# A value product that takes two chunks of keys at a time, and an order of work that prices the change of kind

## What is computed

```python
def attn(q, k, v, heads):            # per example and head, dh = 160 // heads
    sim = q @ k.T * dh ** -0.5
    return softmax(sim, axis=-1) @ v

x = attn(x Wq, ctx Wk, ctx Wv, 20) Wo + bo + x                # unit 0, cross
for block in (L1, L3):
    h = ln(x); x = attn(h q1, h k1, h v1, 20) o1 + x          # units 1 and 5, self
    h = ln(x); x = attn(h q2, ctx k2, ctx v2, 20) o2 + x      # units 2 and 6, cross
    h = ln(x); x = (a * gelu(g)) ff_w2 + x                    # a, g = h ff_w1
    # between L1 and L3 stands L2: 8 heads of 20, keys 508 rows of the context (unit 3),
    # and a small attention of 96 queries over the 256 rows of x (unit 4, "ca")
```

## Time and profile before

| what | value |
|---|---|
| the three runs | 1089.43, 1079.00, 1082.56 us |
| their median | 1082.56 us |
| the profiled execution | 1083.78 us |
| its span on the core | 1082.0 us |
| granted clock, mean of the span | 0.981 |

### The profile page before, as it was taken

One profiled execution on the slowest core, in us unless ns is written; L12 is line 12 of the kernel. 1 busy time (PEld: TensorE's weight loads), 2 busy tenths in 40 slices (PEclk: granted clock), 3 DMA queues, 4 the chain that ended last, 5 costly groups with the idle time before them and its releaser, 6 DMA issues.

```text
span 1082.0 us, 21250 instructions
## 1 busy us (share of the span) xinstructions
PE 1034.7 (96%) x7808; PEld 719.5 (67%) x7808; DVE 689.4 (64%) x1603; ACT 675.4 (62%) x1400; POOL 74.0 (7%) x129
## 2 busy tenths in 40 slices
PE   8999989999998999999998998999999899999978
PEld 5656666667685666767685666676768566765646
DVE  3777757875546567875755775787555556777631
ACT  4556666766664666766765665776665556766641
POOL 3000000000002100001010000000100110000000
PEclk9899999999999999999999999999999999999995
DMA  8110001110232101010113010101021400111000
GB/s 195 42 39 17 21 22 44 30 31 11 49 77 56 25 21 45 21 31 22 35 31 89 21 26 20 45 21 31 10 60 30 103 20 22 34 25 40 11 7 7
DMA packets 31150, 40.26 MB, mean 37 GB/s; under 512 B 10324, under 2 KB 22232, under 8 KB 30728
## 3 DMA queue, kind: packets, MB, share of 16 engines
q1 hardware_dynamic: 31048, 38.89, 14.9%
HBM read 10.97 MB, written 0.66 MB: 11 GB/s over the span
## 4 chain that ended last, share of the span: by engine, by line
PE 87%; DVE 5%; ACT 4%; issue 3%; DMA 0%; POOLq 0%; POOL 0%; DVEq 0%; ACTq 0%
PE st_ps L775 18%; PE pv_ps L831 17%; PE mx_ps L794 17%; PE sp_ps L757 8%; PE sp_ps L758 7%; PE sp_ps L876 4%; PE sp_ps L858 3%; DVE mx L1221 2%; PE sp_ps L808 2%; PE sp_ps L950 2%; PE sp_ps L938 2%; PE sp_ps L989 2%; ACT probs L1062 2%; ACT oT L1069 1%; PE sp_ps L893 1%
## 5 line engine op out<-in xcount | busy, mean ns | idle before, releaser
L1221 DVE TENSOR_REDUCE mx<-mx_ps 128x1 f32<-128x512 f32 (+2 forms) x720 | 475.4, 685 | 184.4 <-PE mx_ps L794 181.1
L1062 ACT ACTIVATE probs<-st_ps 128x512 f32<-128x512 f32 x720 | 400.6, 597 | 184.3 <-PE st_ps L775 178.4
L794 PE MATMUL mx_ps<-ring,qT 128*128 128x512 f32 (+2 forms) x864 | 294.9, 400 | 6.9 <-issue 3.8
L775 PE MATMUL st_ps<-qT,ring 128*128 128x256 f32 (+1 forms) x1408 | 276.1, 298 | 5.4 <-ACT probs L1062 3.2
L775 PEld LDWEIGHTS st_ps<-qT,ring 128*128 128x128 f32 (+1 forms) x1408 | 217.8, 190 | 80.4 <-ACT probs L1062 40.6
L831 PE MATMUL pv_ps<-probs,v 128*9 128x256 f32 (+3 forms) x2944 | 223.8, 377 | 3.0 <-ACT probs L1062 2.3
L794 PEld LDWEIGHTS mx_ps<-ring,qT 128*128 128x128 f32 x864 | 143.5, 190 | 88.9 <-DVE mx L1221 45.7
L831 PEld LDWEIGHTS pv_ps<-probs,v 128*9 128x9 f32 (+2 forms) x2944 | 44.9, 90 | 64.3 <-issue 19.2
L1111 ACT ACTIVATE kdense<-sp_ps 128x512 f32<-128x512 f32 (+2 forms) x116 | 57.4, 539 | 24.4 <-PE sp_ps L876 23.9
L1049 ACT ACTIVATE ks<-sp_ps 128x320 fp32r<-128x320 f32 x80 | 35.2, 440 | 42.3 <-PE sp_ps L858 27.5
L876 PE MATMUL sp_ps<-identr,ks 128*128 128x128 f32 (+1 forms) x416 | 59.7, 279 | 0.7 <-DVE qs L1187 0.6
(11 more groups left out here) (134 smaller groups left out, 1050.2 us busy)
## 6 DMA issues: line engine op xcount, KB each, us to landing
ring<-kdense SPq DMA_DIRECT2D x256, 64.0 KB, 2.0
wb<-in_w_blk SPq DMA_DIRECT2D x4, 1400.0 KB, 9.1
ring<-kdense SPq DMA_DIRECT2D x160, 32.0 KB, 1.8
ring<-kdense SPq DMA_DIRECT2D x32, 127.0 KB, 2.3
wd<-in_w_down SPq DMA_DIRECT2D x4, 400.0 KB, 9.5
ring<-oT SPq DMA_DIRECT2D x16, 64.0 KB, 3.2
ctx_n<-in_ctx SPq DMA_DIRECT2D x4, 192.0 KB, 6.6
x<-in_x SPq DMA_DIRECT2D x4, 160.0 KB, 3.3
```

The source lines that it names most:

```text
L775: mm = pe.matmul(st_ps[s % N_ST][0:kr, i * a["nq"]:(i + 1) * a["nq"]], key_op(n, h)[:, c * P:c * P + kr], query_op(u, b)[:, h // of(u), :] ...
L794: mm = pe.matmul(mx_ps[o % N_MX][0:rows, j * a["nk"]:(j + 1) * a["nk"]], query_op(u, b)[:, h // of(u), tt * P:tt * P + rows], key_op(n, h) ...
L1062: nc.scalar.activation(probs[0:kr, s % N_P, 0:w], st_ps[s % N_ST][0:kr, 0:w], ACT.Exp, scale=float(a["dh"]) ** -0.5).then_inc(S["probs_rea ...
L1221: nc.vector.tensor_reduce(mx[b][0:rows, t, heads[0]:heads[-1] + 1], mx_ps[(o - 1) % N_MX][0:rows, 0:a["hpm"] * a["nk"]].rearrange("p (h k) ...
```

## The change

A value product covers `RUN` = 2 chunks: `runs(u)` gives pairs of chunks, every use of a chunk's number in `plan`, `simulate`, `build` and the TensorE program goes by pairs. Every unit has an even number of chunks, so 368 steps `pv` become 184, each of 16 records. The step waits for the exp of its last slot (the fourth, in unit 4 the second), and each slot still signals by itself when it has been read. `probs` has 7 buffers. In `cost`, `st`, `max` and `pv` have other values, and `simulate` adds `MODE` = 95 ns where a step of TensorE is of another kind (`pv`: "columns", else: "full") than the one before it.

```diff
-N_P = 6
+N_P = 7
 RING = 4
+RUN = 2
 PV_LAG = 2
...
+def runs(u):
+
+    n_c = -(-ATT[u]["nk"] // P)
+    return [list(range(c, min(c + RUN, n_c))) for c in range(0, n_c, RUN)]
...
-        for c in range(q["n_c"]):
-            last = max(s for s in q["slots"] if slots[s]["c"] == c)
-            put(last + PV_LAG, 2, ("pv", n, c))
+        for i, cs in enumerate(runs(q["u"])):
+            last = max(s for s in q["slots"] if slots[s]["c"] == cs[-1])
+            put(last + PV_LAG, 2, ("pv", n, i))
...
-        return 4 + 0.417 * rows, [("dve", 60 + 1.05 * rows)]
+        return 4 + 0.45 * rows, [("dve", 60 + 1.05 * rows)]
...
-        return 218, act(512)
+        return 236, act(512)
     if kind == "pv":
-        return 4 * nq * 0.47, []
+        return len(runs(u)[step[2]]) * nq * 1.57, []
...
+MODE = 95
...
     clock = dict(pe=0, act=0, dve=0, pool=0, dma=0)
+    mode = "full"
+
+    def shape(step):
+
+        return "columns" if step[0] == "pv" else "full"
+
+    def pe_free(step):
+
+        return clock["pe"] + (0 if shape(step) == mode else MODE)
+
...
-            key = (max(start, clock["pe"]), due.get(step)) if cost(step, quads)[0] else (max(start, clock["pe"]), (-10**6, 0, 0))
+            key = (max(start, pe_free(step)), due.get(step)) if cost(step, quads)[0] else (max(start, clock["pe"]), (-10**6, 0, 0))
...
-            t = clock["pe"] = max(start, clock["pe"]) + pe
+            t = clock["pe"] = max(start, pe_free(step)) + pe
+            mode = shape(step)
...
                     elif kind == "pv":
-                        _, n, c = step
+                        _, n, k = step
...
-                        mine = [s for s in quads[n]["slots"] if slots[s]["c"] == c]
-                        if c == 0 and n:
+                        n_c = -(-a["nk"] // P)
+                        mine = [s for s in quads[n]["slots"] if slots[s]["c"] in runs(u)[k]]
+                        if k == 0 and n:
                             pe.wait_ge(S["out_taken"], n)
                         pe.wait_ge(S["probs_ready"], slot_value("probs_ready", mine[-1]))
...
-                        kr = chunk_rows(a["nk"], c)
                         for s in mine:
+                            c = slots[s]["c"]
+                            kr = chunk_rows(a["nk"], c)
                             for i, h in enumerate(slots[s]["heads"]):
...
-                                               start=(c == 0), stop=(c == -(-a["nk"] // P) - 1), tile_position=(0, 32 * j))
-                            if s == mine[-1] and c == -(-a["nk"] // P) - 1:
+                                               start=(c == 0), stop=(c == n_c - 1), tile_position=(0, 32 * j))
+                            if slots[s]["last"]:
                                 mm.then_inc(S["out_full"], 1)
                             else:
                                 mm.then_inc(s_used, 1)
```

More of the change, by code:

```diff
@@ L325, in simulate @@
             streams[4].append(("clear", n))
-        streams[3] += [("pv", n, c) for c in range(q["n_c"])] + [("oev", n)]
+        streams[3] += [("pv", n, i) for i in range(len(runs(q["u"])))] + [("oev", n)]
     last_of, produced = {}, {}
@@ L332, in simulate @@
     for q in quads:
-        for c in range(q["n_c"]):
+        for i, cs in enumerate(runs(q["u"])):
             for s in q["slots"]:
-                if slots[s]["c"] == c:
-                    pv_of[s] = ("pv", q["n"], c)
+                if slots[s]["c"] in cs:
+                    pv_of[s] = ("pv", q["n"], i)
     def needs(step):
@@ L357, in needs @@
         if kind == "pv":
-            return ([("st", max(s for s in quads[step[1]]["slots"] if slots[s]["c"] == step[2]))]
+            cs = runs(quads[step[1]]["u"])[step[2]]
+            return ([("st", max(s for s in quads[step[1]]["slots"] if slots[s]["c"] == cs[-1]))]
                     + ([("oev", step[1] - 1)] if step[1] and step[2] == 0 else []))
         if kind == "oev":
-            return [("pv", step[1], quads[step[1]]["n_c"] - 1)]
+            return [("pv", step[1], len(runs(quads[step[1]]["u"])) - 1)]
         if kind == "kv_proj":
@@ L487, in build @@
         kinds = {step[0]}
-        if step[0] == "pv" and step[2] == -(-ATT[quads[step[1]]["u"]]["nk"] // P) - 1:
+        if step[0] == "pv" and step[2] == len(runs(quads[step[1]]["u"])) - 1:
             kinds.add("pv_last")
@@ L608, in build @@
                 for s in quads[step[1]]["slots"]:
-                    if slots[s]["c"] == step[2]:
+                    if slots[s]["c"] in runs(quads[step[1]]["u"])[step[2]]:
                         if slots[s]["last"]:
@@ L812, in _ @@
                     elif kind == "pv":
-                        _, n, c = step
+                        _, n, k = step
                         u, b, qd = quads[n]["u"], quads[n]["b"], quads[n]["qd"]
                         a = ATT[u]
-                        mine = [s for s in quads[n]["slots"] if slots[s]["c"] == c]
-                        if c == 0 and n:
+                        n_c = -(-a["nk"] // P)
+                        mine = [s for s in quads[n]["slots"] if slots[s]["c"] in runs(u)[k]]
+                        if k == 0 and n:
                             pe.wait_ge(S["out_taken"], n)
                         pe.wait_ge(S["probs_ready"], slot_value("probs_ready", mine[-1]))
-                        if c == 0 and qd == 0:
+                        if k == 0 and qd == 0:
                             last = [s for s in order if s[0] in ("kv_proj", "qkv_proj", "x_keys") and
```

## The result

The changed kernel takes 1120.56 us (median of four runs, 1115.42 to 1123.1) against 1081.9 of the kernel before (median of four runs, one more than ahead of the prediction): 1.034 times as long, 95% interval 1.0275 to 1.0405. The forecast was 1043 us. The profiled execution of after took 1115.42 us with a span of 1113.6. Some executions of a kernel have a clearly lower granted clock and take over 1.5% longer than its fastest; medians and ratios leave them out.

A forecast was written before the change was run, and what follows sets the result against it. TensorE was taken as the bound: span 1082.0 - 49 for fewer changes + 9 for new waits = 1042, plus 1.8 around it and less 1.2 for the median, gave 1043 us, range 1035 to 1053.

The forecast's parts named there:

- Fewer changes: On TensorE, 180 changes to column tiles and back go at 0.30 us each: 54 us, 49 on the chain.
- Longer blocks: A run holds TensorE 1.00 us; full banks give 1.09 us of exp and 1.29 of reduction, covering both engines.
- the 9 us for all new waits: Allowance in the sum for TensorE's new waits, a third more idle than the 31.5 us there were.
- The plan's prices: In the scheduler: new TensorE prices some 6% low, exp 11%, reduction 7%; MODE's effect unreadable, gain bounded at 5 us.
- Seven buffers: For probabilities: three free slots give 1.6 us of exp against 1.00 us of run, so costed at nothing.
- The wait for the last slot: Before each run, TensorE waits for two more exps: nothing to 201 us, expected near today's 2.3 us.
- The rival "slower": TensorE stands at each run's last exp, 420 ns late on 184 runs, 77 us: 1110 us, chance 0.05.
- The sign named for a wrong forecast: In the profile after: TensorE under 93% with `probs` or `mx` in the table of waits.
- What holds TensorE: TensorE, busy 1034.7 of 1082.0 us, bounds the kernel; its savings come off the time if the others keep up.

The follow-up runs named there:

- run2_mode0: The changed kernel with MODE = 0 instead of 95, its new prices kept: 1101.87 us, 1.0163 of the kernel before.
- light kernels: Before and after with exp, reductions or both cut to 64 columns; with both, before took 1066.98 us, after 1031.42 (one execution).
- kernels with three banks: run2_mode0 and the kernel before, each with three banks for scores and two instead of three for the background: 1156.44 and 1168.39 us.
- true prices: The changed kernel with profiled prices of exp, reduction and value product, a change of kind at 145 ns in the clock only: 1116.28 us.

## Why the prediction was wrong, point by point

- *Fewer changes* was right. All 184 runs stand as 16 records; a run takes 0.98 us in the chain against 1.00 forecast. There are 177 bursts fewer (361 - 184), where the text had 180, since the three pairs of two quads no longer stand side by side; they cost 49.0 us less, 0.28 each, where the text had 54 us at 0.30, of them 49 on the chain. 0.20 us behind each was right too.
- *Longer blocks* is the step that failed, and with it the 9 us for all new waits in the sum: 72.9 us were added, and 11.7 at half clock. I set 1.09 us of exp and 1.29 us of reduction against 1.00 us of run, counted on both engines being covered and gave the rest no price of its own. That counts the cover only if the banks have just been filled, and stops at the end of the run. In the rows above the cover held almost to the end of the run, and the time was lost behind it: both engines are empty, TensorE can refill only two banks of each, then it waits for a whole exp or reduction. Four slots of scores and four maxima stand between runs where there were two and two. In run2_mode0 waits are 66 us more (170.3 - 104.2), 58 of them before scores and maxima, 0.36 us for each of 184 runs. The text itself had 0.27 us per run as the point from which it turns slower. That ScalarE's and VectorE's time is the cause is shown by the light kernels; that it is two banks and not, say, the order is argued from the rows and from the kernels with three banks.
- *The plan's prices*: 4 us lost with single chunks, 9 won with runs. But MODE, for which I had no row and no cost, is half of the loss, 19 of 38.7 us. (The text called 3.36 against 2.704 us "a fifth more"; it is a quarter, 24%.) I had written down that value products would lose against anything else that is ready and come later, and then took 9 us for all new waits together, from a share of the idle time there was. Why exactly MODE costs this with runs stays open: waits rise by 7 us and the excess at half clock by 8 against run2_mode0, in one profiled execution each.
- *Seven buffers* was right as far as it was tried: an eighth does nothing with runs, a seventh nothing with single chunks; runs with six were not run. *The wait for the last slot* stayed small, as forecast: TensorE's waits for `probs` at the value product rose from 2.3 us to 9.1.
- *The rival "slower"* came near the time (1110) by another way. Its lateness at each run's last exp isn't what is seen: most waits stand before scores and maxima, behind the run, and true prices don't remove them. The sign named for a wrong forecast came, though: TensorE at 92.7% (1032.4 of 1113.6 us) with `probs` in the table of waits.
- *What holds TensorE*: "busy 96%" was read as "the others have room". ScalarE at 62% and VectorE at 64% do have room, but not, as I read it, the queue to use it: two banks each. With single chunks ScalarE was busy for 87% of the value products' time; that was a resource of the kernel before, and the change spent it.

## What to carry to other kernels

Making a block of work on the fullest engine longer uses up what the queues between the engines hold: before merging, count what the consumers have left at its *end*, and how many rounds of refilling stand before the next block. Here two banks of 0.55 us each did not carry blocks of 1.0 us with four pieces due between them, whatever the mean shares said. And a scheduler that is taught a true cost can get worse: when the price enters the choice of the next step, it changes the order everywhere, so try price and choice apart.

## What the runs showed of the hardware

The change to four column tiles and back costs more than the records of the value product show: in the traces of before and after 0.09 us ahead, 0.10 behind, and 0.10 once more at the second full-array matmul. (Full-array means every matmul without a `tile_position`; ahead of this I wrote that they use all 128 columns, but some of the background have 80 or fewer.) Merged chunks of 256 queries go on at 0.216 us for every four records, 0.43 us a chunk.

The granted clock differed between before (0.981) and after (0.968), and in these traces it fell where TensorE had been idle in part. The table by stage of after (span, then busy us of TensorE, the load of weights, VectorE, ScalarE and GpSimd, the clock, DMA share, GB/s), and its wait at 581 us:

```profile
340.00:348.00 8.00, 5.24 (x43) 3.63 (x43) 7.37 (x18) 1.51 (x4) 3.61 (x5) 0.98 0.00 0
348.00:362.00 14.00, 14.00 (x45) 9.51 (x44) 5.83 (x18) 5.21 (x14) 0.00 (x0) 0.53 0.00 1
...
581.00:588.50 7.50, 0.22 (x2) 0.04 (x2) 0.31 (x3) 1.08 (x2) 0.00 (x0) 0.64 0.83 224
588.50:597.00 8.50, 8.50 (x41) 6.38 (x42) 3.10 (x5) 3.49 (x7) 0.00 (x0) 0.51 0.00 0
```

```profile
588.50 0.77 PE L814 MATMUL mx_ps<-ring,qT 128*128 128x512 f32 x1 [7.28 <-issue]
```

The first two stretches in the kernel before:

```profile
340.00:348.00 8.00, 6.75 (x63) 4.81 (x62) 6.64 (x18) 1.15 (x4) 2.60 (x5) 1.00 0.00 1
348.00:362.00 14.00, 13.49 (x90) 8.54 (x93) 6.65 (x19) 9.84 (x24) 1.81 (x1) 1.00 0.02 4
```

TensorE was busy for 5.24 of 8 us and then had 0.53 of its clock, nearly all at the lower level of 1.2 GHz, for some 14 us, though it was busy in all of them. In the kernel before it had 6.75 of 8 us busy there, in other work, and kept the full clock. At 581 us a wait of 7.28 us ahead of a maximum stood before and in the second fall; the profile names no releaser, and the DMA engines were busy for 0.83 of it. In the kernel before the longest such wait was 3.78 us. So waits went along with a cost at the clock: 11.7 us of the excess counted above, beside 31.6 us by which the span grew, lie in stretches at half clock.
